# A burst of 96 matmuls over zeros, in sixteen 32x32 squares of the array, ahead of TensorE's first work

## The chip, the cores and the metric

The kernel runs on one core of one Trainium2 chip. The metric is the device time of one execution in microseconds (us). The kernel has one launch, float32 data throughout, and TensorE is written `pe`, VectorE `dve` (DVE), ScalarE `act` (ACT), GpSimd `pool` (POOL) and SyncE `sp` (SP).

## The reference, cut to what matters

The input is eight images of 32 channels, 128 by 128. Each goes through two residual blocks behind a group norm:

```python
x = x + _L0_conv_ref(_gn(x), depthwise, pointwise, attention, global_attention)
x = x + _L1_conv_ref(_gn(x), w_off, w_conv, b_conv)
# L0: depthwise 3x3, then three 32x32 channel mixes, two of them softmax weights:
#     one 3x3 convolution once the four are multiplied together
# L1: a 3x3 convolution gives offsets, the image is read at the moved places
#     (bilinear), and a last 3x3 convolution with bias follows
```

The change touches none of this arithmetic. It stands in front of the set-up, in which the L0 weights are multiplied together and the L1 weights are turned and laid out.

## The kernel before, in words

Four rows of an image lie side by side on the 128 partitions (32 channels each), so that a 3x3 convolution is three matmuls over columns shifted by one. `conv_group` makes eight output rows at a time as two halves of 64 output columns of the array, 512 values wide. The first group of an image is made in four strips of 32 columns (`first_group`).

Every engine has its instruction order written out by hand, and semaphores join them. A list `job_order` sets the order of TensorE's jobs. There is one loop over the eight images and in it one over eight chunks of the deformable stage. All of that begins after a head, which is what matters here:

- POOL clears some tiles, makes the identity `ident` and counts `s_setup["pool"]` up. It then waits for the mixed weights `mix_t`, multiplies them out into `w1_base` in 18 small steps (L1078) and sums them (L1082, L1084).
- DVE makes the softmax (L1171 to L1181), and passes three small products back to SBUF (L1185, L1187, L1189). After that, in its own order, stand the statistics of image 0 in two halves (`x_stats`, L1256). Then follow the norm (L1221 to L1246) and the scaled weights `w1` (L1268, L1270).
- PE makes the three small products (L581, L585, L587), each of which waits for DVE. It then makes 18 transposes of the L1 weights (L592 into `off_ps[0]`, L595 into `down_ps`), waits for `w1`, and makes the bias sums (L633) and the first convolution (L616, L620, L606, L608).
- SP and ACT issue the loads of the weights, and SP those of image 0 into `xa`.

The tile `mapped` holds the output of the deformable stage. It is first written by L1127, long after the head, and `off_ps` is first written by L592. `CH` is 512 and `Q` is 32. The waits at the start of PE's program are:

```python
pe.wait_ge(s_setup["pool"], 2)
pe.wait_ge(s_setup["dve"], 2)
```

Of the kernel before, what the change touches and what calls it, by code (L numbers as in the profile page):

```python
# [13 lines left out]
def deformable_preact_kernel(nc, x, dw_w, pw_w, att_w, glob_w, off_w, conv_w, conv_b, out):  # L14
# [8 lines left out]
    Q = C  # L23
# [8 lines left out]
    CH = KR * WQ  # L32
# [68 lines left out]
    with ctx:  # L101
        def sb(name, shape, dt=fp32):
            return ctx.enter_context(nc.sbuf_tensor(name, shape, dt))

        def pb(name, shape):
            return ctx.enter_context(nc.psum_tensor(name, shape, fp32))

        def sem(name):
            return ctx.enter_context(nc.semaphore(name))
# [13 lines left out]
        mapped = sb("mapped", [P, HQ, WQ])  # L123
# [81 lines left out]
        off_ps = [pb(f"off_ps{n}", [P, 2 * CH]) for n in range(2)]  # L205
# [59 lines left out]
        grid_ready = sem("grid_ready")  # L265
        source_loaded = sem("source_loaded")
        source_used = sem("source_used")
        hat_step = sem("hat_step")
        sp_step = sem("sp_step")
        dve_step = sem("dve_step")  # L270
# [305 lines left out]

        @block.tensor
        def _(pe):
            pe.wait_ge(s_setup["pool"], 2)
            pe.wait_ge(s_setup["dve"], 2)  # L580
            nc.tensor.matmul(c_ps[0][0:32, 0:32], soft_e[:, 1, :], ident[0:32, 0:32], start=True, stop=True)\  # L581
# [467 lines left out]

        @block.gpsimd  # L1050
        def _(pool):
            pool.memset(ident, 0.0).then_inc(pool_step, 1)
            pool.memset(centre_tap[:, :], 0.0).then_inc(pool_step, 1)
            pool.memset(minus_one[:, :], -1.0)
# [18 lines left out]
            for rp in range(2):  # L1073
                for ky in range(3):
                    j = rp + ky
                    p = slice(Q * j, Q * j + Q)
                    for kx in range(3):
                        last = pool.tensor_scalar(w1_base[p, kx, C * rp:C * rp + C], mix_t[p, :],  # L1078
                                                  dw_sb[p, 3 * ky + kx:3 * ky + kx + 1], None, ALU.mult)
# [26 lines left out]
            for i in range(NB):  # L1106
                for k in range(NK):
                    n = k % 2
# [27 lines left out]
            for which in END_SHARES[1]["pool"]:  # L1136
                to, rows = end_row(*which, 1)
                last = pool.tensor_copy(to, rows)
# [3 lines left out]
            with pool.If(pool.value_load(is_far[0:1, 0:1], min_val=0, max_val=1) != 0):  # L1142
                pool.iota(index, pattern=[[1, W]], base=0, channel_multiplier=0,
                          allow_small_or_imprecise_dtypes=True).then_inc(grid_ready, 1)
                for wh in range(2):
                    for hh in range(2):
                        q = slice(Q * (2 * wh + hh), Q * (2 * wh + hh) + Q)
# [7 lines left out]
        def _(dve):  # L1155
# [234 lines left out]
            for _, i, m in left_over:  # L1390
                add_group(i, i % 2, i % 3, m, CONV2_GROUPS[m], bank("c2", i, m))
# [108 lines left out]
```

## Time and profile before

| what | value |
|---|---|
| times of three runs | 762.17, 765.5, 766.83 us, median 765.5 |
| span of the profiled execution, first to last instruction | 759.7 us |
| PE busy | 697.8 us (92%) |
| DVE, ACT, POOL busy | 74%, 63%, 65% |
| mean granted TensorE clock | 0.970 |

The span leaves out what lies before the first and after the last instruction. The profiled execution's own time is not given apart. Against the three times shown, 2.5 to 7.1 us lie around its span, 5.8 against the median. The granted clock is a share of full speed: 1.00 stands for 2.4 GHz and 0.50 for 1.2 GHz.

### The profile page before, as it was taken

The page shows a single profiled execution, that of the slowest core. Times are in us where ns is not written, and L with a number is a line of the kernel's source. Part 1 is how long each engine was busy: PE and PEld are TensorE (multiplying, and loading weights), DVE is VectorE, ACT ScalarE, POOL GpSimd, SP SyncE. Part 2 cuts the span into 40 slices and gives each one's busy share as a digit, 9 for nine tenths or more (in the row PEclk, how much of TensorE's full clock was granted, in tenths as well). Part 3 has the DMA queues.
Part 4 walks back from the last instruction along what each step waited for, and adds up shares of the span by engine and source line. Part 5 has one row for each costly group of instructions (what it writes and reads, how often), then busy time and mean ns, then how long its engine had stood idle before and what let it go on. Part 6 is the DMA issues. An engine that isn't in the chain of part 4 may idle for free. (4 is left out here: it accounts for less than half of the span.)

```text
span 759.7 us, 10814 instructions
## 1 busy us (share of the span) xinstructions
PE 697.8 (92%) x3500; PEld 250.0 (33%) x3500; DVE 563.6 (74%) x1031; ACT 478.8 (63%) x841; POOL 490.8 (65%) x434
## 2 busy tenths in 40 slices
PE   4799969998999997999979999899989999998976
PEld 4233323332333332333323333233323333332322
DVE  3687997688976699559976689756995687557692
ACT  7487845884567645666546754776565764777560
POOL 5005955986597654974757646776549657899850
PEclk9999979998999999999989999999999999999998
DMA  8959904999669795899949898597967661576564
GB/s 142 187 92 152 162 3 104 193 150 181 129 151 212 136 205 107 205 165 179 170 111 219 133 196 152 137 215 144 204 120 172 141 143 38 132 135 149 130 145 116
DMA packets 240878, 113.08 MB, mean 149 GB/s; under 512 B 140880, under 2 KB 235184, under 8 KB 239024
## 3 DMA queue, kind: packets, MB, share of 16 engines
q1 hardware_dynamic: 216784, 100.55, 69.1%
q10 hardware_dynamic: 24032, 11.78, 8.9%
q8 instruction: 29, 0.48, 0.3%
q14 instruction: 33, 0.27, 0.1%
HBM read 31.59 MB, written 16.78 MB: 64 GB/s over the span
## 5 line engine op out<-in xcount | busy, mean ns | idle before, releaser
L1317 DVE COPY_PREDICATED other_row<-down_ps,row_diff 128x768 f32<-128x768 int32 x128 | 124.3, 1024 | 132.7 <-ACT down_ps L920 132.6
L1115 POOL TENSOR_TENSOR other_row<-other_row,x_quads 128x512 f32<-128x512 f32 x64 | 76.3, 1192 | 179.3 <-DVE other_row L1329 179.2
L715 PE MATMUL off_ps<-x1a,wo 128*64 128x512 f32 x768 | 183.5, 613 | 7.4 <-DVE other_row L1329 7.4
L606 PE MATMUL c_ps<-mapb,w 128*64 128x512 f32 x336 | 159.9, 619 | 18.4 <-DVE x1a L1301 18.4
L715 PE MATMUL off_ps<-x1b,wo 128*64 128x512 f32 x768 | 176.6, 594 | 0.0
L909 ACT ACTIVATE other_row<-row_diff 128x768 f32<-128x768 f32 x128 | 101.8, 842 | 89.0 <-POOL row_diff L1101 84.2
L606 PE MATMUL c_ps<-xb,w 128*64 128x512 f32 x336 | 151.1, 599 | 5.6 <-DVE x1a L1301 3.8
L608 PE MATMUL c_ps<-xa,w 128*64 128x512 f32 x336 | 151.1, 599 | 0.0
L608 PE MATMUL c_ps<-mapa,w 128*64 128x512 f32 x294 | 140.9, 622 | 0.0
L1101 POOL TENSOR_TENSOR row_diff<-x_quads 128x594 f32<-128x594 f32 x64 | 79.3, 1239 | 40.7 <-ACT x_quads L945 40.7
L920 ACT ACTIVATE down_ps<-off_ps,bias_o 128x512 f32<-128x512 f32 x64 | 41.9, 654 | 95.1 <-PE off_ps L715 55.7
L715 PEld LDWEIGHTS off_ps<-x1b,wo 128*64 128x64 f32 x768 | 56.8, 137 | 111.0 <-issue 111.0
L715 PEld LDWEIGHTS off_ps<-x1a,wo 128*64 128x64 f32 x768 | 56.0, 140 | 110.5 <-issue 100.7
L1121 POOL TENSOR_TENSOR other_col<-other_col,off_abs 128x512 f32<-128x512 f32 x64 | 82.9, 1295 | 5.0
L1127 POOL TENSOR_TENSOR mapped<-other_col,other_row 128x512 f32<-128x512 f32 x64 | 81.8, 1278 | 5.0
L1118 POOL TENSOR_TENSOR other_col<-other_col,other_row 128x512 f32<-128x512 f32 x64 | 81.7, 1276 | 5.0
L606 PEld LDWEIGHTS c_ps<-mapb,w 128*64 128x64 f32 x336 | 45.6, 140 | 112.6 <-issue 89.0
L1116 POOL TENSOR_TENSOR other_col<-other_col,other_row 128x512 f32<-128x512 f32 x64 | 82.0, 1282 | 0.0
L606 PEld LDWEIGHTS c_ps<-xb,w 128*64 128x64 f32 x336 | 45.3, 137 | 100.8 <-issue 93.2
L932 ACT ACTIVATE beyond<-off_abs,minus_one 128x1024 bf16<-128x1024 f32 x64 | 72.9, 1139 | 0.1
L922 ACT ACTIVATE off_abs<-off_ps,bias_o 128x1024 f32<-128x1024 f32 x64 | 70.7, 1105 | 0.0
L1224 DVE TENSOR_SCALAR four_mv<-own_mv,ones 32x2 f32<-32x2 f32 x64 | 56.5, 883 | 2.1
(134 smaller groups left out, 981.8 us busy)
## 6 DMA issues: line engine op xcount, KB each, us to landing
x1b<-x1a SPq DMA_DIRECT2D x28, 520.0 KB, 6.7
mapb<-mapa SPq DMA_DIRECT2D x28, 520.0 KB, 8.2
mapa<-mapped SPq DMA_DIRECT2D x224, 64.0 KB, 2.1
out_dram<-x1a SPq DMA_DIRECT2D x49, 256.0 KB, 4.7
x_quads<-x1a SPq DMA_DIRECT2D x192, 65.0 KB, 3.3
xb<-in_x_dram SPq DMA_DIRECT2D x48, 256.0 KB, 9.1
xa<-in_x_dram ACTq DMA_DIRECT2D x40, 256.0 KB, 6.3
xa<-in_x_dram SPq DMA_DIRECT2D x16, 256.0 KB, 7.0
```

The source lines that it names most:

```text
L606: nc.tensor.matmul(bank[0:64, :], weights[:, kx, :], rows_b[:, 4 * g:4 * g + 4, kx:kx + W], start=(kx == 0), stop=(kx == 2))
L608: last = nc.tensor.matmul(bank[64:128, :], weights[:, kx, :], rows_a[:, 4 * g:4 * g + 4, kx:kx + W], start=(kx == 0), stop=(kx == 2))
L715: last = nc.tensor.matmul(off_ps[k % 2][64 * t:64 * t + 64, CH * n:CH * n + CH], wo[wpar][:, kx, 64 * t:64 * t + 64], rows[:, 4 * k:4 * k ...
L909: act.activation(other_row[n][:, :, KR // 2 * odd:KR // 2 * odd + KR // 2, :], every_other_3(row_diff[n], odd), ACT.Copy)
L932: act.activation(beyond[:, :], off_abs[k % 2][:, :], ACT.Relu, bias=minus_one[:, :], accum_out=far[i % 2][:, k:k + 1]).then_inc(beyond_rea ...
L1101: pool.tensor_tensor(row_diff[n][:, :, :], x1_quads[:, KR * k + 1:KR * k + KR + 2, :], x1_quads[:, KR * k:KR * k + KR + 1, :], ALU.subtrac ...
L1115: step(pool.tensor_tensor(split(column), split(column), own, ALU.add))
L1116: step(pool.tensor_tensor(side, side, other_row[n][:, 0, :, :], ALU.add))
L1118: step(pool.tensor_tensor(side, side, column, ALU.subtract))
L1121: step(pool.tensor_tensor(side, side, off_abs[n][:, 1:2 * CH:2].rearrange("p (h w) -> p h w", h=KR), ALU.mult))
L1127: pool.tensor_tensor(by_pairs(mapped, KR * k, 0), split(side), split(column), ALU.add).then_inc(mapped_ready, 1)
L1317: last = dve.copy_predicated(other_row[n][:, :, KR // 2 * odd:KR // 2 * odd + KR // 2, :], bass.AP(tensor=rows.tensor, offset=rows.offset ...
```

## The change

POOL first clears the first eight rows of `mapped` (128 partitions by 512 values). PE waits for that and then issues three phases of 32 matmuls each, with 32x32 weights and 512 moving columns, all zeros. In a phase each of the sixteen squares (row strip `q`, column strip `c`) gets two matmuls that accumulate in one place. The bank is that of the row strip in phase 0, the next one in phase 1, and `(q + c) % 4` in phase 2. The four banks are the two halves of `off_ps[0]` and `off_ps[1]`. Between phases, and after the last, PE waits for the last matmul of the phase before. Two semaphores are new. Nothing reads the results.

```diff
+        warm_ready = sem("warm_ready")
+        warm_phase = sem("warm_phase")
...
         @block.tensor
         def _(pe):
+            banks = [off_ps[0][:, 0:CH], off_ps[0][:, CH:2 * CH], off_ps[1][:, 0:CH], off_ps[1][:, CH:2 * CH]]
+            zeros = mapped[:, 0:8, :].rearrange("p h w -> p (h w)")
+            pe.wait_ge(warm_ready, 1)
+            for phase in range(3):
+                if phase:
+                    pe.wait_ge(warm_phase, phase)
+                for tap in range(2):
+                    for q in range(4):
+                        for c in range(4):
+                            n = (q + (0, 1, c)[phase]) % 4
+                            last = nc.tensor.matmul(banks[n][Q * c:Q * c + Q, :], zeros[Q * q:Q * q + Q, 0:Q],
+                                                    zeros[Q * q:Q * q + Q, :], start=(tap == 0), stop=(tap == 1))
+                last.then_inc(warm_phase, 1)
+            pe.wait_ge(warm_phase, 3)
             pe.wait_ge(s_setup["pool"], 2)
...
         def _(pool):
+            pool.memset(mapped[:, 0:8, :], 0.0).then_inc(warm_ready, 1)
             pool.memset(ident, 0.0).then_inc(pool_step, 1)
```

PE, the start of its program, before: the three small products stand first (`x n` counts equal instructions in a row).

```order
L577 UNCONDITIONAL_BRANCH [waits barrier_Pool_Activation_PE_DVE_SP_release]
L581 MATMUL c_ps0<-mapa 32x32 [waits setup_dve,setup_pool]
L585 MATMUL c_ps1<-mapa 32x32 [waits l0_weights_loaded,setup_dve]
L587 MATMUL c_ps2<-mapa 128x32 [waits setup_dve]
L592 MATMUL off_ps0<-mapa 128x64 [waits setup_act]
```

PE, the same place, after: the first row of each wait and the rows of phases 0 and 1.

```order
L579 UNCONDITIONAL_BRANCH [waits barrier_Pool_Activation_PE_DVE_SP_release]
L591 MATMUL off_ps0<-mapped 32x512 [waits warm_ready]
L591 MATMUL off_ps0<-mapped 32x512 x7
L591 MATMUL off_ps1<-mapped 32x512 x8
L591 MATMUL off_ps0<-mapped 32x512 x8
L591 MATMUL off_ps1<-mapped 32x512 x8
L591 MATMUL off_ps0<-mapped 32x512 [waits warm_phase]
L591 MATMUL off_ps0<-mapped 32x512 x3
L591 MATMUL off_ps1<-mapped 32x512 x8
```

Everything that stood first now stands behind 96 matmuls and three waits on them. The order behind them is unchanged, and line numbers are 16 higher.

POOL, the start of its program, after, where `mapa` is the tile that `ident` lies in:

```order
L1066 UNCONDITIONAL_BRANCH [waits barrier_Pool_Activation_PE_DVE_SP_gather]
L1068 MEMSET mapped 128x512
L1069 MEMSET mapa 64x64
L1070 MEMSET centre_tap 128x64
L1071 MEMSET minus_one 128x1
```

Before, the row of `mapa` stood directly behind the branch, and all of POOL's work is moved behind one memset.

## Rows read from the trace of the kernel before

**Rows 1.** The page: span, and the queue of code blocks (packets, MB, share).

```profile
span 759.7 us, 10814 instructions
...
q8 instruction: 29, 0.48, 0.3%
```

**Rows 2.** Timeline of the head, POOL: start us, us, engine, line, what, xcount.

```profile
0.74 0.14 POOL L1052 MEMSET mapa<- 64x64 f32 x1 [0.29 <-POOLq L1488]
...
1.22 0.23 POOL L1057 TENSOR_SCALAR_AFFINE_SELECT mapa<-mapa 64x64 f32<-64x64 f32 x1 [0.19 <-POOL centre_tap L1053]
...
1.58 0.41 POOL L1062 MEMSET wo_base<- 128x384 f32 x1
```

**Rows 3.** Timeline of the head, from the first matmul to the first convolution.

```profile
7.14 0.28 PE L581 MATMUL c_ps<-mapa 32*32 32x32 f32 x2 [7.14 <-DVEq L1183]
...
8.61 0.28 PE L585 MATMUL c_ps<-mapa 32*32 32x32 f32 x2 [1.18 <-DMA mapa<-v_depthwise_weights_dram]
...
9.16 0.63 PE L587 MATMUL c_ps<-mapa 32*128 32x32 f32 x2 [0.27 <-DVE mapa L1187]
...
10.12 7.47 POOL L1078 TENSOR_SCALAR w_base<-mapa 32x32 f32<-32x32 f32 x18 [6.90 <-DVE mapa L1189]
10.55 2.47 DVE L1256 BATCH_NORM_STATS2 stats_x<-xa 128x6 f32<-128x512 f32 x4 [0.53 <-DMA xa<-in_x_dram]
...
10.74 4.10 PE L592 MATMUL off_ps<-mapa 64*128 64x64 f32 x18 [0.95 <-ACT mapa L776]
...
14.77 4.04 PE L595 MATMUL down_ps<-mapa 32*128 32x32 f32 x18
...
15.78 2.47 DVE L1256 BATCH_NORM_STATS2 stats_x<-xa 128x6 f32<-128x512 f32 x4 [2.75 <-DMA xa<-in_x_dram]
...
18.07 0.32 POOL L1084 TENSOR_TENSOR w_sum<-w_sum,w_base 128x64 f32<-128x64 f32 x1
...
23.98 0.31 DVE L1268 TENSOR_SCALAR w<-w_base,dve_columns 128x192 f32<-128x192 f32 x1
...
24.60 0.38 PE L633 MATMUL c_ps<-dve_columns,w_sum 128*64 128x1 f32 x4 [5.79 <-DVE w L1270]
```

**Rows 4.** Timeline of PE, rounds of the first convolution, one record per pass.

```profile
24.92 1.06 PE L620 MATMUL c_ps<-xb,w 128*32 128x512 f32 x1
...
25.77 1.06 PE L620 MATMUL c_ps<-xb,w 128*32 128x512 f32 x1
...
28.33 0.78 PE L620 MATMUL c_ps<-xb,w 128*32 128x512 f32 x1
...
28.95 0.59 PE L620 MATMUL c_ps<-xb,w 128*32 128x512 f32 x1
...
29.96 0.59 PE L606 MATMUL c_ps<-xb,w 128*64 128x512 f32 x1
...
30.39 0.59 PE L606 MATMUL c_ps<-xb,w 128*64 128x512 f32 x1
```

**Rows 5.** Stretches of 1 us around PE's longest later stall: PE busy (instructions), granted clock.

```profile
94.00:95.00 1.00, 0.78 (x4) 1.00 0.00 0
...
96.00:97.00 1.00, 0.00 (x0) 0.98 0.00 0
...
101.00:102.00 1.00, 0.73 (x6) 0.50 0.00 0
...
107.00:108.00 1.00, 1.00 (x6) 0.90 0.00 0
```

**Rows 6.** The same view around PE's stall near the end.

```profile
731.00:732.00 1.00, 0.06 (x2) 1.00 0.03 9
...
735.00:736.00 1.00, 1.00 (x4) 0.63 0.20 47
```

**Rows 7.** DMA queues from 28 to 32 us: the first block of that code queue.

```profile
q8 instruction: 1, 0.02, 2.1%
```

**Rows 8.** The DMA view, issues: KB each, median us from issue to landing.

```profile
mapa<-v_depthwise_weights_dram ACTq DMA_DIRECT2D x4, 1.1 KB, 3.8
conv_b_col<-in_L_conv_b_conv_dram SPq DMA_DIRECT2D x4, 0.1 KB, 6.0
```

## The prediction, made before the changed kernel ran

> **What bounds the kernel now.** I read the page first for the span of 759.7 us [rows 1]. The change stands entirely in the first microseconds, so the timeline of the head decides, and there I looked for who waits for whom. PE does nothing for 7.14 us. The burst goes into that hole, and the first question is whether it fits. The head itself ends at 24.60, when the first convolution can start, and PE has waited 5.79 us for DVE's scaled weights by then [rows 3]. So the head is bounded by DVE's chain: the second half of the statistics starts at 15.78, when its data land (2.75 us of waiting for DMA), and from there norm and weights follow without a hole to 23.98 and 24.60 [rows 3]. What comes before 15.78 on PE, POOL and DVE has slack, and what moves 24.60 moves, as a bound, everything behind it one to one.
>
> Second, the clock. The stretches of 1 us show that PE's last work before a stall ended at 94.78 and the granted clock fell from 1.00 to 0.50 (2.4 to 1.2 GHz) at 96.98, 2.2 us later. PE resumed at 101.27 (0.73 of the stretch busy), and the clock came back at 107.2, 5.9 us after that (0.90 over the stretch means 0.2 us at 0.50) [rows 5]. Near the end, work stopped at 731.06 and the clock fell at 735.26, 4.2 us later [rows 6]. In the head the view prints 1.00 throughout, yet the rounds of the first convolution tell another rate: passes over 512 columns follow each other at 0.85 us (24.92 to 25.77), later at 0.43 (29.96 to 30.39) [rows 4]. The first is the lower level. The step of 0.62 us from 28.33 to 28.95 is 0.39 at the slow rate and 0.23 at the fast one, so the clock rose at 28.7, 3.8 us after the convolution began. The slow stretch costs half of its 3.8 us, 1.9 us. That is all a raised clock could give back in the head, since the transposes end at 18.81 with 5.79 us to spare [rows 3].
>
> **The memset.** The nearest row is 128x384 in 0.41 us; 512 columns are 0.41 x 512 / 384 = 0.55 us by proportion. It starts at 0.74 and ends at 1.29, and PE can start at about 1.35. POOL's other set-up work moves by about 0.5 us [rows 2]. It costs nothing, because POOL then stands idle for 6.90 us before L1078, and PE needs the identity only at 7.14 [rows 3].
>
> **The burst.** A float32 matmul makes two passes (the rows count x2 for one), and a pass over 512 columns takes 0.85 us slow or 0.43 us fast [rows 4]. In the first convolution four column strips share a round: PE's next pass of each strip comes 0.85 us later, not 3.4. Whether four row strips also share it, no row shows, since every matmul there uses all 128 rows. I take it that they do and bound it from the other side below. Then a phase is 2 matmuls x 2 passes = 4 rounds, three phases are 12 rounds, that is 10.2 us at the lower level and 5.1 at the higher. At the end of each phase a pass has 0.21 us beyond its round (1.06 against 0.85) [rows 4], and the semaphore costs some 0.19, the nearest row being POOL waiting for its own earlier work [rows 2]. Three times 0.4 is 1.2 us.
>
> If the clock rises 3.8 us after the start: 1.35 + 3.8 + (1 - 3.8/10.2) x 5.1 + 1.2 = 9.6. If 5.9 us: 1.35 + 5.9 + (1 - 5.9/10.2) x 5.1 + 1.2 = 10.6. If it doesn't rise: 1.35 + 10.2 + 1.2 = 12.8. So L581 starts at T, about 10, in place of 7.14. The burst does not fit into the hole; it delays the set-up chain by about 3 us.
>
> **What the delay meets.** L581 to L587 are joined through DVE copies. The step from L585 to L587 is 0.55 us; L585 itself had waited for the depthwise weights, so it now starts at T + 0.55. DVE's third copy ended at 10.02 (0.53 idle before 10.55), 1.41 us after L585, so now at T + 1.96. The first half of the statistics takes 2.47 us and ends at T + 4.43 [rows 3]. It must be done by 15.78, so the delay is free up to **T = 11.35**. Beyond that it costs one to one. POOL starts L1078 1.51 us after L585 and is done with the sum at 18.39, 9.78 us after L585, so at T + 10.33 = 20.3, against 23.98. The transposes take 8.07 us (10.74 to 18.81) and start at T + 1.73, when L587 ends; they end at 19.8, against 24.60 [rows 3]. Both have 3 us or more to spare. At T = 10 all three are covered: cost 0.
>
> **What the clock gives.** By 24.6 PE has been idle again for 4.8 us, and the two falls seen came 2.2 and 4.2 us after work stopped [rows 5, 6]. The transposes do not look like work that raises it: the first nine and the second nine take the same, 4.10 and 4.04 us, although together they last 8 us [rows 3]. So the first convolution starts at the lower level as before: gain 0.
>
> The sum is 759.7 + 0 + 0, with the same 5.8 us around it: **765.5 us**, no change.
>
> **A page that counts the squares differently.** No row here has row strips, as said. The Trainium skill ("TensorE: Matmul & The Clock Gate", Part 3: Packing small matmuls) gives 10.6 times for sixteen 32x32 tiles, not 16. As an estimate by that page, the rounds would be 16/10.6 = 1.5 times as long and T about 12.2, some 0.8 us late. No run here shows it.
>
> **The rivals.**
>
> (a) **The clock stays up.** If the transposes hold the level once the burst has raised it, the fall comes up to 4.2 us after they end; at T = 10 that is 24.0, just short of 24.60, and at T = 10.6 it is 24.6. The whole slow stretch would then go: 765.5 - 1.9 = 763.6. Against it: transposes at the higher level would also end sooner, so that the idle time grows, and one of the two falls seen came after 2.2 us.
>
> (b) **The burst overruns a little.** The clock doesn't rise for it (T = 12.8, 1.45 us late), or its code comes late. The first block of the queue that carries most of the code arrives only between 28 and 32 us [rows 7], and 29 blocks serve the whole program [rows 1]; 96 matmuls make 384 instructions (two passes, each with its weights) beside 7000 (twice 3500), 1.6 blocks more, and they are wanted while image 0 loads. Under this load tiny transfers took 3.8 and 6.0 us [rows 8]. T becomes 13.8 to 16, which is 2.4 to 4.7 us late. The case spans 766.5 to 770.2, with 768 in the middle. Nothing in the trace shows how far ahead PE holds its code.
>
> (c) **The third phase runs one row strip at a time.** There each bank receives from all four row strips, each in its own 32 partitions. If that is refused to run together, the phase is 16 rounds in place of 4. The work counts 8 + 16 = 24 rounds, 20.5 us slow: T = 1.35 + 3.8 + (20.5 - 3.8)/2 + 1.2 = 14.7, or with a rise after 5.9 us 15.8. That is 3.4 to 4.4 us beyond 11.35, a time of 769.4. The Trainium skill ("TensorEngine Tiling (Array Packing)", Gotcha 1: PSUM Pressure) says that different row tiles can't use one bank at the same time. By that rule this rival is what happens; whether it speaks of a bank or of a bank's strip of 32 partitions decides, and no run here shows it.
>
> (d) **Row strips never run together; this is the slower one.** Every phase is 16 rounds, 48 in all, 41 us slow. T = 1.35 + 3.8 + (41 - 3.8)/2 + 1.2 = 24.9, which is 13.6 us beyond 11.35: 779.1 us, 1.8% slower. PE's order is fixed, so L581 stands behind the last phase. DVE stands at L1185 behind that with both halves of the statistics, and POOL at L1078. The point from which a loss of over 1% starts is T = 19, where the delay is 7.65 us. For it is only that no row shows row strips; against it, column strips share rounds cleanly.
>
> **How the numbers follow.** Forecast, covered: 0.70. (a) 0.07, (b) 0.12, (c) 0.06, (d) 0.05. Three runs spread over 4.7 us, 0.6% [times above], so about 1% is what a measurement can tell from no change, and (a) to (c) are all within it. Within 1%: 0.94. Slower: 0.05 from (d). Faster by over 1% would need 7.7 us, four times the most that the clock could give: 0.01. The range takes in (a) to (c) and the spread of the forecast, that is 761.8 to 770.2; only (d) and stray runs stay out.
>
> **What the profile of the changed kernel would show.** The burst starts at 1.3 to 1.4. Passes of one square follow at 0.85 us, then 0.43 after a rise at 5 to 7.5 us. L581 comes at 9.6 to 10.6. The statistics still start at 15.78 behind a DMA, L633 stands at 24.6, and the rounds behind it again have 0.85 us. The granted clock, now recorded, should read 0.50 there and the mean should be below 0.970. I am wrong if L581 comes after 11.35, if L633 moves by more than half a microsecond, if the rounds at 25 us follow at 0.43 us, or if the end moves while L633 doesn't.

## The result, and the profile after

The changed kernel took 767.42 us (median of 18 runs), the kernel before 765.31 on the same chip (18 runs). The ratio is 1.0033 [1.0018, 1.0049]: the change costs 0.3%. Here and below the two numbers in brackets are the 95% interval of the ratio. Repeated later, the changed kernel took 766.77 us, a ratio of 1.0027 [1.0011, 1.0044]. The means differ by 2.2 us in the first comparison (767.63 and 765.39) and by 1.9 in the second (766.98 and 765.09), each uncertain by some 0.6: about 2 us are to be explained. One execution of the changed kernel took 1219.67 us at a mean granted clock of 0.556; it is left out of the ratio, did not come again in twelve later runs, and is not explained.

The profiled execution of after took 767.6 us. The page:

```profile
span 765.8 us, 11199 instructions
...
PE 703.9 (92%) x3692; PEld 249.7 (33%) x3692; DVE 565.2 (74%) x1031; ACT 479.1 (63%) x841; POOL 491.6 (64%) x435
...
q8 instruction: 31, 0.51, 0.3%
```

PE has 192 passes and 192 weight loads more, 384 instructions, and the queue of code has 31 packets for 29 [rows 1]. 0.51 MB in 31 packets is 16 KB each. The spans can't be subtracted: 765.8 against 759.7 [rows 1] is 6.1 us, three times what the times say. The unchanged kernel, profiled again (`base_again` below), had a span of 767.0. Its time and that of the changed kernel's profiled execution are 1.8 us above their spans (768.78 and 767.6), so 759.7 us of span belong to a time of about 761.5, far below the median of 765.3. The first profile was of a short execution, and what the change does has to be read stage by stage, over several traces.

The timeline of the head, after:

```profile
1.32 3.75 PE L591 MATMUL off_ps<-mapped 32*32 32x512 f32 x64 [1.32 <-POOL mapped L1068]
...
5.25 4.75 PE L591 MATMUL off_ps<-mapped 32*32 32x512 f32 x128 [0.17 <-PE off_ps L591]
...
10.06 0.24 PE L597 MATMUL c_ps<-mapa 32*32 32x32 f32 x2
...
11.43 2.22 PE L608 MATMUL off_ps<-mapa 64*128 64x64 f32 x18
...
13.57 2.90 PE L611 MATMUL down_ps<-mapa 32*128 32x32 f32 x18
...
15.99 2.47 DVE L1273 BATCH_NORM_STATS2 stats_x<-xa 128x6 f32<-128x512 f32 x4 [1.89 <-DMA xa<-in_x_dram]
...
19.11 1.27 DVE L1241 TENSOR_SCALAR four_mv<-own_mv,ones 32x2 f32<-32x2 f32 x4
...
25.10 0.38 PE L649 MATMUL c_ps<-dve_columns,w_sum 128*64 128x1 f32 x4 [8.63 <-DVE w L1287]
...
25.42 1.06 PE L636 MATMUL c_ps<-xb,w 128*32 128x512 f32 x1
...
26.27 1.06 PE L636 MATMUL c_ps<-xb,w 128*32 128x512 f32 x1
```

These rows answer to [rows 2 to 4]. A phase has 64 passes, so at 4 rounds sixteen squares share each round. The first phase takes 3.75 us, 4 rounds of 0.85 and a little, so row strips share rounds. The other two take 4.75 together; the third starts at 7.66 and takes no longer than the second. The three small products start at 10.06. The first transposes now take 2.22 us for 4.10 [rows 3]: the clock is up. The statistics start at 15.99 behind the load. L649 stands at 25.10, 0.50 later than L633 did [rows 3], and the rounds after it have 0.85 us again.

The clock rose early. The passes of the second phase, the profile's view of line L591 from 5.2 to 7.6 us (durations in ns, least, median and most):

```profile
L591 PE MATMUL off_ps<-mapped x64: 587/588/612, 5.3 to 7.0; 32*32 32x512 f32 x64
```

That is the higher level, 0.59 us for the 1.06 of a pass at the lower one, so the clock was up at 5.25, at most 3.9 us after the burst began. The trace's record of the clock starts at 4.62 with the higher level (in before it starts at 28.70, where the rounds show the rise), which would be 3.3 us after.

The stretches of 1 us on PE (busy with its instructions, granted clock, DMA share, GB/s) show the clock falling under the transposes:

```profile
14.00:15.00 1.00, 1.00 (x10) 0.93 0.39 57
15.00:16.00 1.00, 1.00 (x6) 0.50 0.03 8
...
28.00:29.00 1.00, 1.00 (x13) 0.74 1.22 195
```

0.93 means that it fell at 14.86, while PE stayed busy until 16.47 (13.57 + 2.90). In the first convolution it rose at 28.5 (0.74 is half a microsecond at 0.50), 3.4 us after its start at 25.10; in before it rose at 28.7.

The head holds 0.4 to 0.6 us of the loss: the start of the first convolution is 25.10 and 25.04 in the two traces of after, 24.60 and 24.52 in the two of before. By the next chunk this can't be told from the scatter: POOL's first L1144 starts at 72.22, the same line of before (L1127) at 72.06 and 72.54. The rest must lie elsewhere. Of the 64 chunks that POOL finishes with this line, the stage from the 60th to the 64th differs. POOL's timeline before:

```profile
694.89 1.27 POOL L1127 TENSOR_TENSOR mapped<-other_col,other_row 128x512 f32<-128x512 f32 x1
...
729.55 1.26 POOL L1127 TENSOR_TENSOR mapped<-other_col,other_row 128x512 f32<-128x512 f32 x1
```

and after:

```profile
697.60 1.26 POOL L1144 TENSOR_TENSOR mapped<-other_col,other_row 128x512 f32<-128x512 f32 x1
...
734.75 1.26 POOL L1144 TENSOR_TENSOR mapped<-other_col,other_row 128x512 f32<-128x512 f32 x1
```

34.66 us have become 37.15. This stage was picked by comparing these two traces; whether it holds in others is a question for the experiments. They come first; then this stage is opened.

### The profile page after: what moved, and what is told of

The parts are those of the page before. It is cut to its first block and busy times, and to the rows that moved or that the text cites. A ratio compares the mean times of both kernels' runs of the same rounds, so it can differ in the third digit from the quotient of the medians.

```text
span 765.8 us, 11199 instructions
## 1 busy us (share of the span) xinstructions
PE 703.9 (92%) x3692; PEld 249.7 (33%) x3692; DVE 565.2 (74%) x1031; ACT 479.1 (63%) x841; POOL 491.6 (64%) x435
## 5 line engine op out<-in xcount | busy, mean ns | idle before, releaser
L731 PE MATMUL off_ps<-x1a,wo 128*64 128x512 f32 x768 | 179.7, 603 | 6.8 <-DVE other_row L1346 6.8
L622 PE MATMUL c_ps<-mapb,w 128*64 128x512 f32 x336 | 162.8, 628 | 20.6 <-DVE x1a L1318 20.3
L624 PE MATMUL c_ps<-mapa,w 128*64 128x512 f32 x294 | 143.8, 633 | 0.0
L1144 POOL TENSOR_TENSOR mapped<-other_col,other_row 128x512 f32<-128x512 f32 x64 | 81.8, 1279 | 5.0
L1241 DVE TENSOR_SCALAR four_mv<-own_mv,ones 32x2 f32<-32x2 f32 x64 | 57.3, 895 | 2.1
```

The source lines that it names most:

```text
L622: nc.tensor.matmul(bank[0:64, :], weights[:, kx, :], rows_b[:, 4 * g:4 * g + 4, kx:kx + W], start=(kx == 0), stop=(kx == 2))
L624: last = nc.tensor.matmul(bank[64:128, :], weights[:, kx, :], rows_a[:, 4 * g:4 * g + 4, kx:kx + W], start=(kx == 0), stop=(kx == 2))
L731: last = nc.tensor.matmul(off_ps[k % 2][64 * t:64 * t + 64, CH * n:CH * n + CH], wo[wpar][:, kx, 64 * t:64 * t + 64], rows[:, 4 * k:4 * k ...
L1144: pool.tensor_tensor(by_pairs(mapped, KR * k, 0), split(side), split(column), ALU.add).then_inc(mapped_ready, 1)
```

## The experiments

**First: which part of the change costs?** `base_again` is the kernel before, unchanged.

> The kernel before, unchanged, as a control: its ratio to itself shows what this comparison can tell apart. All theories expect 1.000 within 0.15%, about 765.3 us. Its trace serves as a second one of the kernel before: if the stalls of TensorE after image 1 and the low stretches of the clock fall elsewhere than in the first trace (span 759.7), the 6.1 us between the two profiled spans are mostly luck of the run, and only about 2 us (0.33%) belong to the change.

764.75 us, 0.9994 [0.9974, 1.0014], span 767.0. The same program has profiled spans that differ by 7.3 us, so the spans of two traces settle nothing here.

`one_phase` keeps 32 of the 96 matmuls, 128 instructions:

```diff
-            for phase in range(3):
+            for phase in range(1):
...
-            pe.wait_ge(warm_phase, 3)
+            pe.wait_ge(warm_phase, 1)
```

> The burst cut to its first phase, 32 matmuls. TensorE is free again at about 5.2 us, so the set-up starts at 7.1 as before. If what costs is the delay of the set-up (set-up theory), this is as before, 765.3 us, and L649 starts at 24.6. If the cost comes from the raised clock, or from the code that is added, a third to the whole of the 2.2 us stays: 766 to 767.5 us.

766.64 us, 1.0021 [1.0003, 1.0039]. A third of the burst, which ends long before anyone wants PE, still costs about two thirds of the loss by the medians (the interval is wide). Its first convolution starts at 24.45, not late, so nothing of this is made in the head.

`code_only` keeps all 96 matmuls with 8 columns for 512, so that the instructions are there and the work is not:

```diff
-                            last = nc.tensor.matmul(banks[n][Q * c:Q * c + Q, :], zeros[Q * q:Q * q + Q, 0:Q],
-                                                    zeros[Q * q:Q * q + Q, :], start=(tap == 0), stop=(tap == 1))
+                            last = nc.tensor.matmul(banks[n][Q * c:Q * c + Q, 0:8], zeros[Q * q:Q * q + Q, 0:Q],
+                                                    zeros[Q * q:Q * q + Q, 0:8], start=(tap == 0), stop=(tap == 1))
```

> The same 96 matmuls, phases and waits, but 8 columns wide instead of 512: the code that TensorE has to fetch is that of the change, the array does next to nothing. TensorE is free at about 5 to 7 us. If the 384 added instructions cost something, by moving the places where code blocks arrive in the whole program, the full 2.2 us stay (767.5 us). If the delay or the clock costs, this is as before, 765.3 us within 0.15%.

766.68 us, 1.0021 [1.0000, 1.0043]. The three small products stand at 7.15 as before:

```profile
7.15 0.28 PE L597 MATMUL c_ps<-mapa 32*32 32x32 f32 x2 [3.29 <-DVEq L1200]
```

so the delay of the set-up isn't needed for a loss. The head isn't untouched, though: image 0's data land later in this trace (the second half of the statistics starts at 16.50, for 15.78 before) and the convolution starts at 25.50, 0.9 us late. So this run doesn't say where the loss is made.

`delay_only` has no burst; PE waits for two POOL clears instead:

```diff
+            pe.wait_ge(warm_ready, 1)
             pe.wait_ge(s_setup["pool"], 2)
...
+            pool.memset(mapped[:, :, :], 0.0)
+            pool.memset(x1_quads[:, 0:60, :], 0.0).then_inc(warm_ready, 1)
             pool.wait_ge(s_setup["dve"], 5)
```

> No burst: TensorE waits at the start for two long clears on GpSimd (mapped and 60 rows of x1_quads), so that the set-up starts at about 10 us as behind the burst, with no matmul before it and no code added. If the delay of the set-up costs, through the weight products on GpSimd that now run beside the statistics of image 0, L633 starts 0.3 to 0.6 us later and the time is 0.3 to 2.5 us above the kernel before. If the cost belongs to the raised clock or to the code, the time is as before, within 0.15%.

766.47 us, 1.0020 [0.9996, 1.0043]. Its head:

```profile
12.00 0.28 PE L584 MATMUL c_ps<-mapa 32*32 32x32 f32 x2 [12.00 <-DVEq L1188]
...
13.91 4.83 DVE L1261 BATCH_NORM_STATS2 stats_x<-xa 128x6 f32<-128x512 f32 x8
...
25.44 0.38 PE L636 MATMUL c_ps<-dve_columns,w_sum 128*64 128x1 f32 x4 [1.73 <-DVE w L1275]
```

With T = 12.00, 0.65 beyond 11.35, the two halves of the statistics join (x8, no wait for the load) and the convolution stands at 25.44, 0.9 late. The prediction's T and its bound of 11.35 hold. For the changed kernel's T of 10.06 this cause gives nothing. The expectation gave this kernel a loss only if the delay costs; its median is 1.4 us up with an interval that takes in no loss, and a convolution 0.9 us late is enough for it.

**Second: does the loss come in the head?** Five kernels compute only two images and leave the other six out. The edit, on before, after, `code_only`, `one_phase` and (below) `six_big`:

```diff
-    NB, C, H, W = x.shape
+    NB, C, H, W = 2, *x.shape[1:]
```

> The kernel before with two of the eight images (the loops over images and the output of the other six are left out). In the full traces the offset set in the head was carried unchanged to the end of image 1 and the traces scattered by up to 4 us only from image 2 on. So this form should scatter less from run to run than the full one (762 to 769 us), about 200 us long, and show an effect of the head in tenths of a microsecond. It is the base of the three beside it.

> The changed kernel with two of the eight images (the other six are left out). If the change costs in the head (0.3 us through statistics that run beside the weight products, 0.2 us through a later load), it is 0.2 to 0.8 us above the two-image form of before, and the rest of the 2.2 us arises behind image 1. If it costs the full 2.2 us already here, the head does it all. If nothing is left (within 0.1 us), the whole cost lies in where later stalls and clock changes meet.

> The form with 96 matmuls of 8 columns, two images only. Its full trace had the data of image 0 landing 0.7 us later (16.50 against 15.78) and an offset of 1.9 us at the first chunk. If the added code delays the loads of image 0 as a rule, this is 0.7 to 1.9 us above the two-image form of before. If that was luck of one run, it is within 0.2 us of it.

> One phase of the burst, two images only. TensorE is free before the softmax is ready, so the head is not delayed: if the head sets the cost, this equals the two-image form of before within 0.2 us (the full trace had an offset of -0.2 us). If the raised clock or the code cost by themselves, it lies 0.5 us or more above.

Medians of 4 runs: 229.71, 231.09, 231.18 and 230.11 us. That looked like a loss of 1.4 us made in the head. Their traces say otherwise: at the 15th chunk `short_after` is 0.08 us ahead of `short_before` (187.79 and 187.87), and the 1.5 us between their spans (229.3 and 227.8) appear behind PE's stall from 197 to 203 us, where the clock stays low for 6.8 us instead of 3.4. Only `short_code_only` is late at the 15th chunk, by 1.2 us. A shorter program has another end. These runs told that in this form the head of the change is not what costs, and nothing of how the full kernel loses its time.

**Third: the same work with little code.** `six_big` does 12 rounds with six matmuls over the whole array, 24 instructions:

```diff
+            zeros = mapped[:, 0:8, :].rearrange("p h w -> p (h w)")
+            pe.wait_ge(warm_ready, 1)
+            for tap in range(6):
+                nc.tensor.matmul(off_ps[1][:, 0:CH], zeros[:, 0:128], zeros, start=(tap == 0), stop=(tap == 6 - 1))
...
+            pool.memset(mapped[:, 0:8, :], 0.0).then_inc(warm_ready, 1)
```

> The burst as 6 matmuls over the whole array (128x128 weights, 512 columns, zeros) in place of 96 in squares: the same 12 rounds, so TensorE is busy from 1.3 us to about 9.5 and the clock rises and falls as with the burst, but with 24 instructions of code added and not 384. If the added code costs the 2.2 us, this is within 0.15% of the kernel before (765 us). If the raised clock and the later set-up cost, it is at 767 to 767.6 us, like the change.

> The same 6 matmuls over the whole array, two of the eight images only (the other six are left out). The two-image forms were 229.7 us (before), 230.1 (one phase, 128 instructions), 231.1 (change) and 231.2 (code only). The code theory expects 229.5 to 230.0; the clock-and-set-up theory 230.8 to 231.4.

764.46 us, 0.9995 [0.9975, 1.0016]; two images 230.46 (5 runs, 229.15 to 231.58, too wide to tell). Its row:

```profile
1.32 8.19 PE L584 MATMUL off_ps<-mapped 128*128 128x512 f32 x12 [1.32 <-POOL mapped L1058]
```

PE is as busy in the hole as in the change, T is 9.44, and there is no loss: the convolution starts at 24.51. So neither the work of the burst nor what it does to the clock is the cause; what is left is the number of instructions. The times alone say this only just: the interval and that of `after_again`, taken beside it, touch (1.0016 and 1.0011).

`late_fill` puts three such matmuls behind the transposes, directly ahead of the first convolution, with the same memset on POOL:

```diff
             transpose_l1_weights()
+            zeros = mapped[:, 0:8, :].rearrange("p h w -> p (h w)")
+            pe.wait_ge(warm_ready, 1)
+            for tap in range(3):
+                nc.tensor.matmul(off_ps[1][:, 0:CH], zeros[:, 0:128], zeros, start=(tap == 0), stop=(tap == 3 - 1))
```

> Three matmuls over the whole array with zeros, placed behind the transposes, in TensorE's hole from 18.8 to 24.6 us, with no burst at the start: 5.1 us at the low clock, done before the scaled weights of image 0 are there. If a raised clock at the start of the first convolution is worth what the rows say (the slow stretch of 3.4 to 5 us costs half of itself), the time is 1.5 to 2.5 us below the kernel before, about 763 us. If what is won in the head is lost in later stalls, it is as before.

761.6 us, 0.996 [0.9939, 0.998].

```profile
18.74 4.75 PE L727 MATMUL off_ps<-mapped 128*128 128x512 f32 x6
...
24.85 0.62 PE L622 MATMUL c_ps<-xb,w 128*32 128x512 f32 x1
...
25.30 0.59 PE L622 MATMUL c_ps<-xb,w 128*32 128x512 f32 x1
...
27.81 0.36 ACT L871 ACTIVATE x1a<-c_ps,bias 32x128 f32<-32x128 f32 x1 [2.68 <-PE c_ps L626]
```

The convolution's first rounds now follow at 0.45 us. ACT's first eviction stands at 27.81, at 29.74 in before: the 1.9 us that the prediction named as all that a raised clock gives back in the head. The medians show more, 3.5 us here and 2.9 in the repeat below; the intervals reach down to 1.5 and 0.8, so 1.9 is inside both, and whether there is anything beyond it stays open.

`after_again` is the change once more, beside them.

> The changed kernel again, unchanged. If the first comparison (ratio 1.0033) holds, it is 767 to 767.8 us against some 765 of the kernel before on the same chip; if part of it was the choice of runs, the ratio is 1.001 to 1.002. Its trace shows whether L649 starts 0.2 to 0.6 us later than in the kernel before as a rule.

766.77 us, 1.0027 [1.0011, 1.0044].

**Fourth: is it the code, and where?** `two_blocks` adds 32 matmuls of 8 columns and a fourth wait behind the burst, 512 instructions in all:

```diff
             pe.wait_ge(warm_phase, 3)
+            for tap in range(2):
+                for q in range(4):
+                    for c in range(4):
+                        last = nc.tensor.matmul(banks[q][Q * c:Q * c + Q, 0:8], zeros[Q * q:Q * q + Q, 0:Q],
+                                                zeros[Q * q:Q * q + Q, 0:8], start=(tap == 0), stop=(tap == 1))
+            last.then_inc(warm_phase, 1)
+            pe.wait_ge(warm_phase, 4)
```

> The changed kernel with 32 more matmuls, 8 columns wide, behind the burst: 512 added instructions, two whole code blocks (16 KB each) and not one and a half, so that in the rest of the program the blocks arrive beside the same work as in the kernel before. TensorE is free some 0.8 us later than with the change. If the places of the code blocks behind the head cost the rest, only the head's 0.4 us stay: 765.0 to 765.8 us against 765.1 of before. If not, this is at 767 us or above, like the change.

768.56 us, 1.0038 [1.0008, 1.0068].

```profile
10.81 0.33 PE L598 MATMUL off_ps<-mapped 32*32 32x8 f32 x31
...
12.66 0.36 PE L598 MATMUL off_ps<-mapped 32*32 32x8 f32 x33 [1.52 <-issue]
...
13.20 0.24 PE L604 MATMUL c_ps<-mapa 32*32 32x32 f32 x2 [0.18 <-PE off_ps L598]
...
26.59 0.38 PE L656 MATMUL c_ps<-dve_columns,w_sum 128*64 128x1 f32 x4 [3.67 <-DVE w L1294]
```

In the middle of the tiny matmuls PE stands 1.52 us with nothing to wait for but its own code. A packet of the code queue, q8, came from 9.88 to 11.26 us, and PE goes on 1.4 us after it. That is rival (b) as it was written, caught in another kernel: T = 13.20, 1.85 beyond 11.35, and the convolution 2.0 us late. The expectation of 765.0 to 765.8 us missed this. Its stage from chunk 60 to 64 is short, 34.73. So this kernel loses in the head what the change loses at the end.

`code_mid` leaves the head alone and puts 96 matmuls of 8 columns into PE's stall at 95 us:

```diff
+                if isinstance(i, int) and i == 2:
+                    for tap in range(24):
+                        for c in range(4):
+                            nc.tensor.matmul(ps[Q * c:Q * c + Q, 0:8], wo_base[:, 0, Q * c:Q * c + Q],
+                                             wo_base[:, 1, 0:8], start=(tap == 0), stop=(tap == 23))
```

> The kernel before with 96 matmuls, 8 columns wide, put where TensorE waits from 94.8 to 101.3 us for the weights of image 2 (they read finished weight tiles and write the bank of the job behind them). The head is untouched, 384 instructions are added and executed in a hole. If the places of code blocks behind the head cost, this is 1 to 2 us slower than before (ratio 1.0015 to 1.0025). If the code costs only where its block loads beside image 0, this is as before within 0.15%.

766.62 us, 1.0021 [0.9995, 1.0047] from 6 runs. The matmuls themselves are hidden:

```profile
95.11 1.79 PE L660 MATMUL c_ps<-wo_base 128*32 128x8 f32 x192
```

`both_fills` is `late_fill` with nine matmuls of 384 columns in that same stall:

```diff
+                if isinstance(i, int) and i == 2:
+                    for tap in range(9):
+                        nc.tensor.matmul(ps[:, 0:3 * P], wo_base[:, 0, :], wo_base[:, :, :],
+                                         start=(tap == 0), stop=(tap == 8))
```

> The filling behind the transposes (ratio 0.996 alone) and, besides, 9 matmuls of 384 columns over finished weights in TensorE's stall from 94.8 to 101.3 us, 5.8 us at the high clock, so that the clock should stay up where the rows of before have it low from 97.0 to 107.2. PE was at half speed for 5.9 us of work there: 2.9 us less if all of it reaches the end, that is 759 to 760 us, ratio 0.992 to 0.993. If later stalls take it back, it stays at 0.996. If the filling runs into the moment when the weights are ready, it is above 0.996.

762.13 us, 0.9965 [0.9938, 0.9992]. Locally it does what it should: L721 takes 2.78 us for its 12 passes,

```profile
92.59 6.07 PE L661 MATMUL c_ps<-wo_base 128*128 128x384 f32 x18
...
99.21 2.78 PE L721 MATMUL off_ps<-x1a,wo 128*64 128x512 f32 x12
```

(the first row is the fill, two passes each), where the same 12 passes of `late_fill` take 5.26. The end doesn't come sooner than in `late_fill`, and the 759 to 760 us that were expected at best are missed. The next stall takes the gain back: PE waits 4.14 us for DVE's `other_row` there, in `late_fill` 1.56, and both go on together, at 119.44 and 119.59.

**Fifth: repeated, and with two whole blocks.** `late_fill_again` and `code_mid_again` are the same kernels once more.

> The filling behind the transposes again, unchanged, to narrow its interval (0.9939 to 0.998). If the gain holds at the size of the head's offset in its trace, -1.9 us, the ratio is 0.9975; if the first comparison stands, 0.996.

> The kernel before with 96 matmuls of 8 columns in TensorE's stall at 95 us, again, unchanged. The first comparison was 1.0021 with an interval over 1 (0.9995 to 1.0047). If 384 added instructions cost by moving the code blocks behind them, it is again 1.0015 to 1.0025; if not, 0.999 to 1.001, and the residue behind the head has nothing to do with the places of the blocks.

761.63 us, 0.9963 [0.9936, 0.999], and 766.81 us, 1.0032 [1.0011, 1.0053] from 12 runs. So 384 instructions in the middle cost what the change costs, with the head untouched.

`mid_two_blocks` has 128 tiny matmuls in the stall, 512 instructions (`range(24)` becomes `range(32)`).

> The same with 128 matmuls of 8 columns, 512 added instructions, two whole code blocks: behind the stall every block arrives beside the same work as in the kernel before. If the places of the blocks cost and code_mid_again is slower, this is at 1.000 (0.999 to 1.001). If added code costs wherever and however much, it is at 1.002 or above.

764.84 us, 0.9996 [0.9976, 1.0017]. That is what the expectation gave if the places of the blocks cost. More code in the same place, and no loss, although PE waits 2.16 us for it there (the q8 packet came from 96.70 to 97.67, again 1.4 us ahead):

```profile
99.05 0.66 PE L660 MATMUL c_ps<-wo_base 128*32 128x8 f32 x57 [2.16 <-issue]
```

## Where the time goes: one block of code at 685 us

SP issues the second-half moves of the last image, 16 DMAs in a row, which stand on the chain that ended last. The chain after:

```profile
685.19 1.72 SPq L416
...
692.18 2.08 DMA mapa<-mapped
...
694.96 6.50 DMA mapb<-mapa
```

and before:

```profile
683.79 0.61 SPq L414
...
688.36 2.06 DMA mapa<-mapped
...
691.12 6.48 DMA mapb<-mapa
```

After, fifteen of the issues take 0.61 us each and one takes 1.72; before, all sixteen take 0.61. The DMA queues from 684 to 688 us say what is beside it, after:

```profile
q1 hardware_dynamic: 1276, 0.31, 31.2%
q8 instruction: 1, 0.02, 2.2%
```

and before:

```profile
q1 hardware_dynamic: 1698, 0.41, 40.1%
```

A block of code comes in just then. In before, the blocks on either side of these issues come at 672.2 and 700.5. The whole row of issues in SP's timeline, before:

```profile
678.56 10.41 SPq L414 DMA_DIRECT2D mapa<-mapped  x16
```

after:

```profile
681.28 11.51 SPq L416 DMA_DIRECT2D mapa<-mapped  x16
```

`mid_two_blocks`, which adds more code than the change:

```profile
680.74 10.42 SPq L414 DMA_DIRECT2D mapa<-mapped  x16
```

That long issues stand beside arriving blocks shows beyond this place too. This line, with its number in each kernel, issues 3360 DMAs in the 15 full-length traces. 112 of them overlap in time with an arriving 16 KB packet of q8, and 59 of these take over 0.9 us; of the other 3248, 19 do. Before has such an issue too, where a block comes at 558.8 (least, median and most in ns):

```profile
L414 SPq DMA_DIRECT2D mapa<-mapped x4: 610/612/1220, 559.0 to 561.6; - x4
```

PE waits for what these moves and the next one bring, before the second convolution of the last group. Before:

```profile
697.74 0.48 PE L616 MATMUL c_ps<-mapb,w 128*32 128x384 f32 x1 [1.03 <-DMA mapb<-mapa]
```

after:

```profile
701.59 0.82 PE L632 MATMUL c_ps<-mapb,w 128*32 128x384 f32 x1 [3.88 <-DMA mapb<-mapa]
```

In after the clock falls in this wait. Stretches after:

```profile
700.00:701.00 1.00, 0.00 (x0) 0.97 0.82 170
701.00:702.00 1.00, 0.41 (x4) 0.50 0.90 211
...
704.00:705.00 1.00, 1.00 (x14) 0.82 0.95 248
```

Before, PE's gap ended in the stretch from 697 to 698, and the clock was up there and stayed up to 735 (it had been low from 690.9 to 694.3, ahead of the 60th chunk):

```profile
697.00:698.00 1.00, 0.26 (x4) 1.00 0.86 199
```

So in this trace the block costs SP 1.1 us, PE stands longer for it, the clock falls at 700.94, and the passes behind the wait take 0.82 us for 0.48.

Over all full-length traces (us, from rows like those shown):

| kernel | instructions added | block at, us | SP's 16 issues | stage 60 to 64 | of it 62 to 63 |
|---|---|---|---|---|---|
| after, after_again | 384 | 685.1, 685.0 | 11.51, 11.44 | 37.15, 37.10 | 11.48, 11.45 |
| code_only | 384 | 688.1 | 11.11 | 37.03 | 11.36 |
| one_phase | 128 | 685.3 | 11.02 | 36.95 | 11.31 |
| code_mid, code_mid_again | 384 | 682.9, 682.6 | 11.55, 11.61 | 37.08, 38.42 | 11.44, 12.75 |
| before, base_again | 0 | none | 10.41, 10.40 | 34.66, 36.37 | 8.98, 10.71 |
| delay_only | 0 | none | 10.41 | 34.77 | 9.06 |
| six_big | 24 | none | 10.40 | 36.29 | 10.61 |
| late_fill, late_fill_again | 12 | none | 10.41, 10.40 | 34.69, 36.29 | 8.99, 10.62 |
| both_fills | 48 | none | 10.41 | 36.01 | 10.34 |
| two_blocks, mid_two_blocks | 512 | none | 10.41, 10.42 | 34.73, 34.72 | 9.06, 9.06 |

The six traces with a block there (of four kernels) have a mean of 37.3 us and no value under 36.95; the nine others a mean of 35.4 and none over 36.37: 1.9 us. All of it lies in the step from the 62nd chunk to the 63rd; the three other steps of the stage agree within 0.05 us in all 15 traces. 128 and 384 added instructions put the block at the same place and 512 put it back, so the places repeat with about 256 instructions. From the first chunk to the 60th both kinds take the same on average (624.72 and 624.65 us), but single traces scatter there from 622.8 to 626.7, so that a difference of up to about 1.5 us would not be told; from the 64th to the end they agree too (30.7 and 30.6). As far as these means go, the 1.9 us of this stage make up nearly all of the 1.9 to 2.2 that were measured, and the head's 0.4 to 0.6 is hardly seen at the end.

The others fall into two kinds by the clock. Where it fell in this stage (`base_again`, `six_big`, `late_fill_again`, `both_fills`) the step from 62 to 63 takes 10.3 to 10.7 us, where it didn't, 9.0 to 9.1. Which of the two a run is, is luck: `before` and `base_again` are one program. `base_again` shows a wait of 2.77 us at this place without any block,

```profile
702.16 0.82 PE L616 MATMUL c_ps<-mapb,w 128*32 128x384 f32 x1 [2.77 <-DMA mapb<-mapa]
```

and its rounds are slow as well, while `delay_only` waits 2.84 us with the clock up. Without a block the wait is 1.03 to 2.84 us; with it, 3.34 to 3.93 in all six, and the clock falls in all six. So the 1.9 us have two parts: a trace with a block is some 0.8 us (11.3 to 11.5 for 10.3 to 10.7; one has 12.75, where the clock stayed low twice as long) above one without that has the fall too, and the rest is that the fall, worth 1.6 us, comes in six traces of six instead of four of nine.

Shown is that added PE instructions alone cost the time, in the head or in the middle, and 512 of them in the same place do not; that the time is lost between these two chunks; and that a code block lies beside these issues in every trace with the longest steps and in no other. That an arriving block goes with a long issue is shown by all the traces together; how it does so is not, and no kernel moved the block and nothing else. In the times alone, the intervals of `code_mid_again` and `mid_two_blocks` still overlap a little (the near ends are 1.0011 and 1.0017). Not tried: `late_fill` with added code.

## Why the prediction was wrong

**The hole and T: right, in part by luck.** 12 rounds, T forecast at 9.6 to 10.6, measured 10.06. Two terms were off and partly cancel: the clock rose sooner than either case of the sum, and the ends of the phases came to about 2.0 us for 1.2 (10.06 less 1.32, 3.3 of slow rounds and 3.45 of fast ones, an estimate with the rise at 4.62). Squares in four row strips share rounds like column strips, in the third phase too, where one bank receives from four row strips, each in its own 32 partitions. That ends rivals (c) and (d). The Trainium skill's rule of one bank for one row tile ("TensorEngine Tiling (Array Packing)", Gotcha 1: PSUM Pressure) doesn't hold for a bank as a whole here, and its 10.6 for sixteen tiles ("TensorE: Matmul & The Clock Gate", Part 3: Packing small matmuls), by which T was estimated at 12.2, is less than these squares reached.

**What the delay meets: right.** Free up to 11.35 and one to one beyond; `delay_only` and `two_blocks` had 0.65 and 1.85 beyond it and were 0.9 and 2.0 late.

**The clock: right where it mattered.** It rose 3.3 us after the burst began by the trace's record, and at most 3.9, where the prediction had 3.8 to 5.9. The transposes did not hold it, and the convolution began at the lower level. Rival (a) fell because its condition, that the transposes hold the clock, did not come true: it fell under them, at 14.86.

**The head's sum of 0: nearly.** It was 0.4 to 0.6, and little of it was left at the first chunk. The load of image 0 came 0.2 us later (15.99 for 15.78), and DVE's L1241 took 1.27 us for 0.97 beside POOL's weight products, which now run until 19.3. Both are seen in the trace, not separated by a run.

**"The sum is 759.7 + 0 + 0": this is the step that failed.** The prediction counted "1.6 blocks more" of code under rival (b) (384 instructions) and priced them only where PE might stand for them, in the head. It took every block behind the head for free. But blocks are fetched throughout the program, and about one and a half blocks ahead of them move where each of them falls, against a chain whose slack varies. One fell beside SP's issues at 685 us, where nothing covers it. The missing term is 1.9 us: that block made one issue 1.1 us longer, PE's wait behind it grew to 3.88 us, and the clock fell in it. The prediction's last test, "I am wrong if the end moves while L633 doesn't", is nearly what happened.

**The span as the basis** did no harm to the forecast, since the sum was made with its own 5.8 us. But those 5.8 us are no fixed part of a time: where both are known, 1.8 us lie around the span. The 759.7 us belonged to a short execution, and a difference of two spans would have told of 6 us where there are 2.

**The size against the spread.** The measured 0.33% is well inside the 1% band and the range. The forecast of no change is wrong in that repeated runs can tell 2 us from none.

## What to carry to other kernels

Count added instructions as code to be fetched, and ask of each later place with tight DMA issue whether a block of it may now fall there (128 and 384 instructions cost 1.6 to 2.2 us here, 512 in the middle nothing that can be told); compare forms of the same work by their number of instructions (six whole-array matmuls cost nothing where 96 squares cost 2). In this kernel the warming paid only where dense work followed at once: the same kind of burst directly ahead of the first convolution made the kernel 0.4% faster (761.6 us), in front of an idle stretch nothing. Where profiled spans of one program differ by 7 us, compare stages over several traces, not two spans.

## What the runs showed that was not expected

- PE can run out of code. With matmuls of 8 columns it stood 1.52 us in `two_blocks` and 2.16 us in `mid_two_blocks`, with nothing else to wait for, and went on 1.4 us after a code packet had come in.
- Transposes of 32 and 64 columns don't hold the clock: it fell at 14.86, 4.9 us after the last dense pass and 1.6 us before PE became idle.
- Sixteen squares cost the same round as one whole-array pass: rounds of squares start 0.85 us apart at the lower level (1.32, 2.18, 3.03) and 0.43 at the higher, passes of `six_big` 0.85 (2.34, 3.19, 4.04) and 0.43. The sums, 8.68 and 8.19 us, can't be compared as they stand: `six_big` has one end for three, and its clock rose later, with the seventh pass.
- A DMA issue of 0.61 us took 1.63 to 1.81 us beside an arriving block of code (1.30 and 1.23 in `code_only` and `one_phase`). Over all traces 59 of 112 issues of this line beside such a block took over 0.9 us, and 19 of 3248 others.
